# Graph layers, experts and mixture on one core: rows of the last layernorm kept in SBUF, another order of the normalise steps, layer weights prepared during routing

## The reference

```
x = x + L0_gnn(layernorm(x))      # graph attention, 8 heads of 32
x = x + L0_ffn(layernorm(x))      # 16 experts, the best two per node
x = x + L1_gnn(layernorm(x))      # three graph attention layers, one head
x = x + L1_ffn(layernorm(x))      # a feed-forward for the nodes of largest weight
```

```
h = x @ W;  s = h @ a_src;  d = h @ a_dst
alpha = leaky_relu(s[src] + d[dst], 0.2)
out = softmax of alpha over each dst's edges, applied to h[src], + b;  x = gelu(out)
```

## Time and profile before

| | us |
|---|---|
| median of 3 runs (lowest, highest) | 3983.88 (3979.65, 3987.48) |
| the profiled execution: its own time | 3981.09 |
| its span, first to last instruction | 3979.4 |
| start of the first node stage | 483.58 |
| start of `project_phase` (heads) | 523.29 |
| start of the second node stage | 2040.14 |
| start of routing | 2093.84 |
| start of projection | 2545.21 |
| start of the three layers | 2602.52 |
| start of the third node stage | 3740.47 |
| start of the mixture | 3781.69 |

### The profile page before, as it was taken

How to read it: one execution, slowest core, us unless ns; L and a number is a source line. 1 busy time by engine, 2 the same in 40 slices (tenths; PEclk the granted TensorE clock), 3 DMA queues, 4 the chain that set the end, 5 groups by cost and what they waited for, 6 DMA issues and landing times. The chain is left out here.

```text
span 3979.4 us, 69742 instructions
## 1 busy us (share of the span) xinstructions
PE 3475.2 (87%) x27387; PEld 2710.1 (68%) x27388; DVE 2905.3 (73%) x4461; ACT 2380.6 (60%) x3691; POOL 217.9 (5%) x212
## 2 busy tenths in 40 slices
PE   4999748888888898888865999789999999999799
PEld 2555435666666666666654899778887888888577
DVE  6999839999999999999955222366556565655485
ACT  3777628888888888888840011256655665444432
POOL 0000000000000000000001444200000000000010
PEclk9999969999999999999966999899999999999899
DMA  1222331111112311111136898432323322333210
GB/s 47 98 98 98 118 102 51 69 52 66 55 63 107 139 61 57 64 54 66 52 127 201 234 240 233 107 116 100 114 82 114 114 98 81 130 114 120 75 55 33
DMA packets 158629, 398.36 MB, mean 100 GB/s; under 512 B 26555, under 2 KB 104766, under 8 KB 140766
## 3 DMA queue, kind: packets, MB, share of 16 engines
q1 hardware_dynamic: 137592, 368.93, 26.6%
q0 software_dynamic: 13888, 20.07, 2.8%
q10 hardware_dynamic: 6822, 4.85, 0.4%
HBM read 328.61 MB, written 65.19 MB: 99 GB/s over the span
## 5 line engine op out<-in xcount | busy, mean ns | idle before, releaser
L932 PE MATMUL hd_psT<-ident,hd_scores 128*128 128x128 f32 (+1 forms) x5000 | 738.6, 286 | 31.9 <-ACT hd_scores L835 31.9
L844 ACT ACTIVATE hd_probsT<-hd_psT 128x768 f32<-128x768 f32 (+1 forms) x800 | 648.2, 835 | 188.9 <-PE hd_psT L932 187.9
L880 DVE SCALAR_TENSOR_TENSOR hd_scores<-hd_el,hx 128x3136 f32<-128x3136 f32 x200 | 695.7, 3478 | 24.3 <-DMA hd_mask<-mask_dram 18.3
L884 DVE CUSTOM_DVE_ANT_0 hd_scores<-hd_scores,hd_mask 128x3136 f32<-128x3136 f32 x200 | 684.1, 3421 | 8.6
L946 PE MATMUL hd_psO<-hd_probsT,hx 128*32 128x128 f32 (+1 forms) x10000 | 583.5, 286 | 100.5 <-ACT hd_probsT L844 99.7
L932 PEld LDWEIGHTS hd_psT<-ident,hd_scores 128*128 128x128 f32 (+1 forms) x5000 | 544.6, 143 | 185.8 <-issue 183.3
L835 ACT ACTIVATE hd_scores<-hd_scores,hd_negmax 128x1664 f32<-128x1664 f32 (+1 forms) x400 | 640.7, 1602 | 10.6 <-DVE hd_negmax L884 10.4
L1394 PE MATMUL ly_psO<-hx_a,ly_probsT 128*128 128x256 f32 x2500 | 583.6, 381 | 0.0
L1352 ACT ACTIVATE ly_probsT<-ly_psT 128x768 f32<-128x768 f32 (+1 forms) x300 | 249.3, 831 | 469.2 <-PE ly_psT L1383 469.1
L946 PEld LDWEIGHTS hd_psO<-hd_probsT,hx 128*32 128x32 f32 (+1 forms) x10000 | 322.9, 110 | 299.5 <-ACT hd_probsT L844 175.8
L1394 PEld LDWEIGHTS ly_psO<-hx_a,ly_probsT 128*128 128x128 f32 x2500 | 453.6, 189 | 71.3 <-issue 16.6
(11 more groups left out here) (309 smaller groups left out, 3695.7 us busy)
## 6 DMA issues: line engine op xcount, KB each, us to landing
ly_mask<-mask_dram SPq DMA_DIRECT2D x75, 1568.0 KB, 6.7
hd_mask<-mask_dram SPq DMA_DIRECT2D x50, 1568.0 KB, 7.0
moe_w<-in_L_ffn_w SPq DMA_DIRECT2D x144, 512.0 KB
mask_dram<-logc SPq DMA_DIRECT2D x200, 196.0 KB, 1.9
hd_el<-el_dram SPq DMA_DIRECT2D x5, 1568.0 KB, 10.0
hd_el<-el_slope_dram SPq DMA_DIRECT2D x4, 1568.0 KB, 12.9
hd_el<-el_dram ACTq DMA_DIRECT2D x3, 1568.0 KB, 18.4
y_dram<-hd_y_stage POOLq DMA_DIRECT2D x50, 64.0 KB, 6.1
```

The costliest lines, as they stand in the source:

```text
L844: nc.scalar.activation(pT[:, gi % 2, 0:w], psT[gi % 2][:, 0:w], ACT.Copy).then_inc(s_ev, 1)
L880: nc.vector.scalar_tensor_tensor(sc[:, c, :], el[:, h, 0, :], hx[:, b, o:o + 1], el[:, h, 1, :], ALU.subtract, ALU.min).then_inc(s_lk, 1)
L884: nc.vector.tensor_tensor_reduce(out=sc[:, c, :], in0=sc[:, c, :], in1=mask[:, B % 2, :], scale=1.0, scalar=3.0e38, op0=ALU.add, op1=ALU.m ...
L932: last = nc.tensor.transpose(psT[gi % 2][0:r, t * P:(t + 1) * P], sc[:, u % 3, c0:c0 + r], g["ident"][:, :])
```

## The change

- `node_phase`: where `y_in` is given (n1), part p is normalised right behind its own deviation, ahead of `add(p + 1)`; where it is not (n0, n3), it is normalised behind `add(p + 1)`. In both, one part earlier than before.
- n3 no longer stores x3; its x is a tile that stays in SBUF through the mixture, as `res`. The DRAM tensor `x3` and `load_nodes` are gone, and with them the zeroing of the last block of `res` and SyncE's wait for it in `mod_phase` (the node stage zeroes that block). GpSimd's add waits for nothing but its own instructions.
- The layers' weights `wx` live from ahead of the experts' stages on; their loads and preparation move from `node_project_phase` to `router_phase`: on SyncE behind the store of the loop terms and ahead of w3, on TensorE between rank and selector products, on ScalarE behind its exponential.

```diff
@@ node_phase, VectorE
                     stats(p)
                     deviation(p)
-                    if p:
-                        normalise(p - 1)
+                    if y_in is not None:
+                        normalise(p)
                     if p + 1 < NPART:
                         add(p + 1)
-                normalise(NPART - 1)
+                    if y_in is None:
+                        normalise(p)
@@ node_project_phase, SyncE (ScalarE's weights(l) and TensorE's loop over l are taken out alike)
-            for l in range(LAYERS):
-                sp.dma_start(wx[l][:, :, 0:D], a[f"L1_gnn_W{l + 1}"].rearrange("(k p) n -> p k n", p=P)).then_inc(s_w[l], 16)
-                for i, n in enumerate(("as", "ad")):
-                    sp.dma_start(av[:, l, :, i:i + 1], a[f"L1_gnn_{n}{l + 1}"].rearrange("(k p o) -> p k o", p=P, o=1),
-                                 allow_slow_non_contiguous=True).then_inc(s_a[l], 16)
             for p in range(NPART):
@@ router_phase, SyncE
             sp.dma_start(diagonal(g, L1_LOOPS, DROP_R, DROP_Q), dv[:, :].rearrange("p (q o) -> p q o", o=1),
                          allow_slow_non_contiguous=True).then_inc(s_dout, 16)
+            for l in range(LAYERS):
+                sp.dma_start(wx[l][:, :, 0:D], a[f"L1_gnn_W{l + 1}"].rearrange("(k p) n -> p k n", p=P)).then_inc(s_w[l], 16)
+                for i, n in enumerate(("as", "ad")):
+                    sp.dma_start(av[:, l, :, i:i + 1], a[f"L1_gnn_{n}{l + 1}"].rearrange("(k p o) -> p k o", p=P, o=1),
+                                 allow_slow_non_contiguous=True).then_inc(s_a[l], 16)
             for e in range(XE):
@@ router_phase, TensorE
             last.then_inc(s_rank, 1)
+            for l in range(LAYERS):
+                pe.wait_ge(s_w[l], 16)
+                if l:
+                    pe.wait_ge(s_wx, 4 * l)
+                for k in range(2):
+                    for m in range(2):
+                        last = nc.tensor.transpose(psW[k][:, m * P:(m + 1) * P], wx[l][:, m, k * P:(k + 1) * P], g["ident"][:, :])
+                    last.then_inc(s_wT, 1)
+                pe.wait_ge(s_wTc, 2 * l + 2)
+                pe.wait_ge(s_a[l], 32)
+                for k in range(2):
+                    for m in range(2):
+                        last = nc.tensor.matmul(psW[k][:, D:D + 2], wT[:, m, k * P:(k + 1) * P], av[:, l, m, :],
+                                                start=m == 0, stop=m == 1)
+                    last.then_inc(s_wa, 1)
             for i in range(2):
                 pe.wait_ge(s_sel, i + 1)
@@ mod_phase, SyncE, GpSimd and VectorE
-            sp.wait_ge(s_k, 3)
-            load_nodes(sp, res, x3, s_res)
...
-            pool.wait_ge(s_k, 3)
+            pool.wait_ge(s_k, 2)
...
-            pool.wait_ge(s_res, 32)
             nc.gpsimd.tensor_tensor(res[:, :, :], res[:, :, :], xn[:, :, :], ALU.add).then_inc(s_sum, 1)
...
-            nc.vector.memset(res[:, FULL, :], 0.0).then_inc(s_k, 1)
@@ program
+        wx = [sb(f"wx_{l}", [P, 2, R1]) for l in range(LAYERS)]
...
-        node_phase(nc, g, "n3", xt, x_in=x1, y=y, gelu=True, x_out=x3, xn_out=xn)
-        mod_phase(nc, g, xt, xn, y, a, x3, out)
+        x = sb("x3", [P, NB, D])
+        node_phase(nc, g, "n3", xt, x_in=x1, y=y, gelu=True, xn_out=xn, x_tile=x)
+        mod_phase(nc, g, xt, xn, y, x, a, out)
```

More of the change, by code:

```diff
@@ L1138, in _ @@
         def _(pe):
-            for l in range(LAYERS):
-                pe.wait_ge(s_w[l], 16)
-                if l:
-                    pe.wait_ge(s_wx, 4 * l)
-                for k in range(2):
-                    for m in range(2):
-                        last = nc.tensor.transpose(psW[k][:, m * P:(m + 1) * P], wx[l][:, m, k * P:(k + 1) * P], g["ident"][:, :])
-                    last.then_inc(s_wT, 1)
-                pe.wait_ge(s_wTc, 2 * l + 2)
-                pe.wait_ge(s_a[l], 32)
-                for k in range(2):
-                    for m in range(2):
-                        last = nc.tensor.matmul(psW[k][:, D:D + 2], wT[:, m, k * P:(k + 1) * P], av[:, l, m, :],
-                                                start=m == 0, stop=m == 1)
-                    last.then_inc(s_wa, 1)
-            pe.wait_ge(s_wx, 4)
             def transpose_x(b):
@@ L1506, in router_phase @@
         s_w3 = sem("s_w3")
+        av = sb("a", [P, LAYERS, 2, 2])
+        wT = sb("wT", [P, 2, D])
+        psW = [ctx.enter_context(nc.psum_tensor(f"rt_w{i}", [P, 512], F32)) for i in range(2)]
+        s_wT, s_wTc, s_wa, s_wx = (sem(n) for n in ("s_wT", "s_wTc", "s_wa", "s_wx"))
+        s_w = [sem(f"s_w{l}") for l in range(LAYERS)]
+        s_a = [sem(f"s_a{l}") for l in range(LAYERS)]
         psw = ctx.enter_context(nc.psum_tensor("rt_ps_within", [P, 512], F32))
@@ L1574, in _, with weights @@
             nc.scalar.activation(lg[:, :, :], lg[:, :, :], ACT.Exp).then_inc(s_e, 1)
+            def weights(l):
+                for k in range(2):
+                    act.wait_ge(s_wT, 2 * l + k + 1)
+                    if l:
+                        act.wait_ge(s_wa, 2 * l)
+                    nc.scalar.activation(wT[:, k, :], psW[k][:, 0:D], ACT.Copy).then_inc(s_wTc, 1)
+                for k in range(2):
+                    act.wait_ge(s_wa, 2 * l + k + 1)
+                    nc.scalar.activation(wx[l][:, k, D:D + 1], psW[k][:, D + 1:D + 2], ACT.Copy, scale=1.0 - SLOPE).then_inc(s_wx, 1)
+                    nc.scalar.activation(wx[l][:, k, D + 1:R1], psW[k][:, D:D + 1], ACT.Copy, scale=-1.0).then_inc(s_wx, 1)
+            for l in range(LAYERS):
+                weights(l)
         @block.vector
@@ L1819, in mod_phase @@
 @phase
-def mod_phase(nc, g, xt, xn, ff, a, x3, out):
+def mod_phase(nc, g, xt, xn, ff, res, a, out):
     with ExitStack() as ctx:
@@ L1844, in mod_phase @@
         WCOLS = NP // WCHUNKS
-        res = sb("res", [P, NB, D])
         tmp = sb("tmp", [P, 2, D])
@@ L2046, in program @@
             el = [sbl(f"el_{i}", [P, 2, NS]) for i in range(2)]
[L2047 removed]
             mask = sbl("ly_mask", [P, 2, NS])
[L2049 removed]
+            node_project_phase(nc, g, x1, wx, hxa, el[0], mask)
             layers_phase(nc, g, wx, (hxa, hxb), el, mask, y, a)
```

45 lines of the change are left out of this document (10 added, 35 removed).

## The result

| | before | changed kernel |
|---|---|---|
| median of 7 runs (lowest, highest) | 3979.65 (3974.78, 3987.48) | 3964.57 (3962.25, 3968.48) |
| the profiled execution: its own time | 3981.09 | 3968.48 |
| its span | 3979.4 | 3966.8 |

The ratio of the runs is 0.9961, with a 95% interval of 0.9949 to 0.9973: 15.1 us faster by the medians.

A forecast was written before the change was run, and what follows sets the result against it. The kernel was taken as a row of barrier-closed stages, each touched stage bounded by its inner waits. Terms -5.0 - 5.7 + 0.7 + 3.0 = -7.0 us gave 3974.1 or 3976.9, middle 3975.5, range 3968 to 3982.

The forecast's parts named there:

- Part 1: Third node stage: without the store of x3 the mixture starts at 3776.6, not 3781.69: -5.0 us (bounds -5.9, -4.0).
- the 1.84 assumed: Third node stage: one more normalise ahead of the last deviation moves it 1.84 us later, a price read in the second.
- Part 2: Layer weights leave projection, rows load first: projection -5.7 us (-4.9 to -6.4), routing cost 0.
- Part 3: New normalising order in the other node stages: first +0.7 us, second 0, routing +3.0 through a later gate_b.
- the whole normalise: First node stage: upper bound of the new order's cost, +1.9 us.
- the price of the third stage: Third node stage: the new order ends ScalarE 0.65 us later; the first node stage's +0.7 took the same distances.
- The estimate of +4.4: Routing: gate_b's delay by the skill page, +2.4 + 2.0 us, making the sum 1.4 us worse; not adopted.
- Rival A: Routing: the queue does not delay gate_b, so +3.0 goes: -10.0 us, 3972.5; chance 0.15.
- B: New waits eat the projection or third-stage gain: half of 10.7 is left, sum -1.7 us, 3980.8; chance 0.12.
- C: Projection: TensorE's clock stays at half; with no rise at all sum +22 us, 4004; chance 0.07.
- D: Third stage ends by something else than the store, or a barrier's cost is in the semaphores: 0 +- 3; chance 0.04.
- the two halves: Forecast's 0.62 split at the 8 us noise edge: half with A faster, 0.47; half with B and D same, 0.46.

The follow-up runs named there:

- the later groups: The kernel before, unchanged, run again beside the follow-up experiments in groups of 26 to 28 runs: medians 3980.88, 3981.34 and 3981.24.

## Why the prediction was half right

**Part 1, third node stage, -5.0, measured -6.0** (x3 alone -5.5), just outside its bound of -5.9. The last deviation moved back by 1.4 us (30.44 us after the stage's first load, 29.00 before), near the 1.84 assumed. But ScalarE's last ten copies started only 0.3 later instead of 0.6 and took 3.73 us instead of 4.22: TensorE now waited for ScalarE's copies (2.25 us) and not ScalarE for TensorE's transposes (1.08 us before). So ScalarE ended 0.2 earlier against the stage's start and not 0.65 later. The barrier cost its 0.8. Inside the mixture, cost 0 as said.

**Part 2, projection, -5.7, measured -6.1.** The terms stand in the rows above: 5.4 for the rows, 0.9 from TensorE being free, 0.35 back through the clock. In routing the moved work cost nothing in routing, as said.

**Part 3.** First node stage +0.7, measured +1.4 and +1.6: within its bounds, nearer to the whole normalise than to the price of the third stage: the last deviation came 3.0 us later against the stage's start and not 1.84, ScalarE's copies of part 3 started 1.9 later and took 0.5 less, and its loop terms stand behind them. Second node stage 0 and routing +3.0: measured +0.1 and +3.0, with the store of x1 6.1 us later as worked out. The estimate of +4.4 by the Trainium skill ("DMA: Bandwidth & Descriptors", the sections on queues and on the anatomy of a DMA) was too high; the wait grew by 3.1. The Trainium skill gives its 2.0 us for a DMA issued by GpSimd, and gate_b's is SyncE's. Rival A, that the queue delays nothing, is out.

**The step that failed** is in part 2: the moved weights were costed in the two stages where they leave and arrive, and the experts' stage between them was left at 0, on the ground that "a change in one stage moves the end by what that stage gets shorter", because a barrier closes each. A barrier passes on times, but not only those: the position in TensorE's instruction stream passes too, and with it the moment of each fetch. In place of 0 the stage gave -4.8 in the profile, 3.7 of it from the first to the tenth add, and before with 77 instructions more, which changes nothing but that position, was 6.7 faster by the medians. With the edited stages alone the forecast would have held: 3979.65 - 7.9 = 3971.8 lies in its range. The forecast also took the lengths of the untouched stages as fixed. The head of the experts' stage, where tiles took 7 to 9 us instead of 5.52, stood in the trace of before, and the argument never looked at it. How the position works on the stage past the first fetch stays open, as said above. A further 2.5 us lie in which executions were profiled. The parts add up: x3 alone -6.1, weights alone -11.4, order alone +1.3, together -16.2, against 15.1 measured (16.7 if before is taken at the 3981.3 of the later groups). As each part is known to some 5 us only, that they add up this closely is in part luck. In the chances the two halves are swapped by 0.01 (0.31 + 0.15 is 0.46, not 0.47); nothing hangs on it.

Rivals B, C and D did not come: no gain was halved, the clock rose 5.6 us after the first transpose, and the third stage had ended with its store, as its -6.0 shows.

## What to carry to other kernels

A stage that no edit touches can still change, if it runs at the edge of its DMA engines: look for the stretches where a regular loop misses its own pace, and widen the range by them, to both sides. When code moves from one side of such a stage to the other, the engine's later instruction fetches can move with it, as they did here by 77 of 256 instructions; a pad of satisfied waits on that engine tells such an effect from one of the work itself. And where a prefetch and small latency-bound DMAs share the engines, it is worth trying to run less far ahead: 4 tiles instead of 8 gave 14.3 us here.

## What the runs showed of the hardware

- TensorE's instructions come by DMA in packets of 16 KB on a queue of their own, one per 256 instructions (77 + 179 more shifted the packets by one whole place), 12 to 20 us apart in this loop, and one that coincided with a gather and an add at 350 to 390 GB/s went with landings 1.2 and 1.4 us later (5.7 to 6.9, 7.0 to 8.4).
- A disturbed pipeline of gather, products and add does not recover at once: with 64 equal tiles at 5.52 us, the kernel with x3 alone needed 27 tiles to fall back into step, and lost 17 us against before's profile.
- An 8 KB load issued behind a store that fills the queues landed for its user after 5.65 us, against 2.54 with the queue nearly drained.
